# Two chained cross-attention layers on one core: stores between the refills, a first pair by half loads, a later statistics product, and a last attention copy split by bank

## The chip, the cores and the metric

The kernel runs on one core of one Trainium2 chip. The metric is the device time of one launch in microseconds (us). The kernel before took 365.97 us (median of 3 runs, 365.94 to 367.44). Times in the profile come from one further, profiled execution of 364.66 us.

## The reference, cut to what matters

For each of 32 batch elements there are two matrices of 128 channels by 1024 columns, `x` and `y` (the context). Layer 0 is a cross attention in both directions over channels, layer 1 a second one followed by a normalisation over the whole element:

```python
# layer 0, 8 heads of 16 channels; softmax over channels (16 x 16 per head)
attn = softmax(einsum('bhni,bhnj->bhij', q, k) * 16 ** -0.5)
res  = einsum('bhnd,bhde->bhne', v, attn)
x1   = (x + proj_p2r(res_p2r)) + (y + proj_r2p(res_r2p))
# layer 1: queries and keys from y, values from x1
scores = einsum('bhdl,bhel->bhde', Wq y + bq, Wk y + bk) / sqrt(128)
o      = Wo (softmax(scores) (Wv x1 + bv)) + bo + x1
out    = (o - mean(o)) * rsqrt(var(o) + 1e-5) * gn_w[:, None] + gn_b[:, None]
```

Since every attention matrix is channels by channels, the scores need only the 128 x 128 products y·yT and x·yT (summed over the 1024 columns) and the row sums of y. All later weights can then be multiplied together, so that `o` is P·x + Q·y with two 128 x 128 matrices per element.

## The kernel before, in words

The 32 elements are worked on in 16 pairs. One call of `step(h, u, front, middle, back)` on each engine is one step of a pipeline of three parts: **front** transposes the pair's 1024 columns in eight chunks and sums the products in the bank `gacc` (`gram_chunks`, L310); **middle** makes the scores, the softmax and the matrices P and Q of the pair before (`u_products`, `scores`, `z_products`, `m_products`, `pq_products`); **back** forms P·x + Q·y of the pair before that, takes its statistics, normalises it and stores it. Step 0 is (0, 0), step 1 is (0, 1), steps 2 to 15 run in a loop (two to a turn) with all three parts, steps 16 and 17 drain. Each engine has its own instruction order, written out by hand in its `step`; engines meet at semaphores only.

- **SP** issues every DMA, in order, from one queue. There are four slots of buffers (`raw`, `y_blocks`, `xy_hi`, `xy_lo`, `res`); a step uses two. Once a slot's splits and transposes are done, it is refilled with x, four blocks of y, and y for the step after the next (L234 to L247). Both refills come before the two stores of the step (L248 to L259).
- **PE** (TensorE) transposes x (and in step 0 also y) through the bank pair `tpx`; the column chunks of the transposes take every eighth column (L295). In a step, the small product `group_moments` (L352), which averages the statistics over the channels, stands ahead of `m_products` (L414 to L420). PE starts the next pair's `u_products` (L364) when ACT has copied the second `gacc` to `gram`.
- **ACT** (ScalarE) copies the transposes (`xt_out`, L502), `gacc` (`gram_out`, L556), the attention products (`z_out`, L541 and L542), the high part `pq_hi` of P and Q (L547), and the output halves (`out_to_sbuf`, L572); it rounds x and y to their high parts (`split_high`, L565), takes the exponent (L537), makes the scale and shift of the normalisation (`norm_scale`, L524 and L527) and applies it (L586).
- **DVE** (VectorE) transposes the y blocks (L705), does the softmax around the exponent, the statistics (L716 to L764) and the low part `pq_lo` (L709).
- **POOL** (GpSimd) makes the low parts of x and y in pieces (L919) and the power -1/2 of the variance (L926).

For float32 accuracy each output half is made of six products: the high and low parts of x and y with the high part of P and Q, then the high parts with the low part of P and Q.

## Time and profile before

| what | value |
|---|---|
| median of 3 runs | 365.97 us |
| the profiled execution | 364.66 us |
| its span in the trace | 362.9 us |
| PE busy | 334.8 us (92% of the span) |
| PE weight loads busy | 279.7 us (77%) |
| ACT busy | 249.4 us (69%) |
| DVE busy | 243.7 us (67%) |
| POOL busy | 188.8 us (52%) |
| DMA, all queues | 67.43 MB, mean 186 GB/s |
| granted PE clock over the core's span | 0.995 |

How to read it: the span runs from the first to the last recorded instruction; what is missing to the execution's time lies around it. PE is the engine that is busy nearly all the time, so the time can be read as a sum of what PE does and of the places at which it stands idle. "L297" is line 297 of the kernel. In a timeline a row's second number is busy time; since instructions overlap in the pipeline, two neighbours may overlap by some tens of nanoseconds, and differences are best taken from start to start.

### The profile page before, as it was taken

To read this page: it belongs to the slowest core of one execution; us is meant where nothing else is said; L and a number is where in the kernel's file an instruction comes from. 1 tells how busy PE (TensorE), PEld (TensorE's weight loads), DVE (VectorE), ACT (ScalarE), POOL (GpSimd) and SP (SyncE) were. 2 spreads that over 40 slices of the span, in tenths; PEclk is the share of its full clock that TensorE was granted. 3 is DMA by queue.
4 is the path that set the end of the run, shared out by engine and by line. 5 is a ranking of instruction groups with operands and counts; after the bars stand their busy time and mean duration, and the time that the engine had idled before them with its cause. 6 is when DMAs were issued, how large, how long until landed. Compare 5 with 4: busy or idle time off the path is not lost.

```text
span 362.9 us, 8203 instructions
## 1 busy us (share of the span) xinstructions
PE 334.8 (92%) x2646; PEld 279.7 (77%) x2646; DVE 243.7 (67%) x620; ACT 249.4 (69%) x414; POOL 188.8 (52%) x277
## 2 busy tenths in 40 slices
PE   5975999997999999999999999999999999999681
PEld 3864978886797988888897988888797888877470
DVE  1444586774958677694958677694958678593763
ACT  2375486864877787777877786777877686786423
POOL 0079675480845739192846648182845728193001
PEclk9999999999999999999999999999999999999997
DMA  7765545557575565657575665656575756302023
GB/s 246 259 176 167 162 145 166 175 175 271 174 267 173 205 211 151 240 168 268 173 269 175 232 210 170 232 162 246 174 269 175 269 177 220 134 0 116 2 104 128
DMA packets 30410, 67.43 MB, mean 186 GB/s; under 512 B 2368, under 2 KB 17984, under 8 KB 30400
## 3 DMA queue, kind: packets, MB, share of 16 engines
q1 hardware_dynamic: 30400, 67.30, 55.5%
q8 instruction: 5, 0.08, 0.1%
q14 instruction: 5, 0.04, 0.0%
HBM read 50.52 MB, written 16.78 MB: 185 GB/s over the span
## 4 chain that ended last, share of the span: by engine, by line
PE 56%; DVE 16%; SPq 13%; issue 5%; DMA 4%; POOL 3%; ACT 2%; POOLq 0%; DVEq 0%; ACTq 0%
PE gacc L320 19%; SPq L214 8%; PE oacc L340 5%; PE oacc L345 5%; PE oacc L341 5%; PE tpx L297 4%; DVE hstat L716 4%; SPq L208 4%; PE mid L428 3%; POOL xy_lo L919 3%; PE mid L364 3%; DVE mom L740 3%; DMA out<-res 2%; DVE t L705 2%; PE mid L414 2%
## 5 line engine op out<-in xcount | busy, mean ns | idle before, releaser
L919 POOL TENSOR_TENSOR xy_lo<-raw,xy_hi 128x256 fp32r<-128x256 f32 x256 | 177.7, 733 | 130.4 <-ACT xy_hi L565 130.4
L320 PE MATMUL gacc<-t 128*128 128x257 f32 x512 | 124.9, 386 | 3.2 <-DVE attn L814 2.6
L320 PEld LDWEIGHTS gacc<-t 128*128 128x128 f32 x512 | 92.6, 191 | 17.1 <-DVE attn L814 3.0
L705 DVE STREAM_TRANSPOSE t<-y_blocks 128x512 f32<-128x512 f32 x60 | 68.1, 1135 | 3.0 <-DMA y_blocks<-in_ctx 3.0
L565 ACT ACTIVATE xy_hi<-raw 128x1024 fp32r<-128x1024 f32 x64 | 67.4, 1056 | 3.9 <-DMA raw<-in_ctx 3.9
L340 PE MATMUL oacc<-xy_hi,pq_hi 128*128 128x512 f32 x124 | 51.9, 419 | 4.3 <-ACT res L572 2.2
L572 ACT ACTIVATE res<-oacc 128x512 f32<-128x512 f32 x60 | 35.9, 598 | 21.6 <-DMA out<-res 10.5
L341 PE MATMUL oacc<-xy_lo,pq_hi 128*128 128x512 f32 x124 | 48.8, 394 | 0.0
L716 DVE BATCH_NORM_STATS2 hstat<-res 128x6 f32<-128x512 f32 x60 | 39.4, 678 | 13.9 <-ACT res L572 13.9
L502 ACT ACTIVATE t<-tpx 128x512 f32<-128x512 f32 x64 | 38.2, 598 | 12.7 <-PE tpx L297 11.9
L297 PEld LDWEIGHTS tpx<-cst,raw 128*128 128x128 f32 x256 | 36.3, 192 | 4.4 <-DMA cst<-in_consts 1.3
L345 PE MATMUL oacc<-xy_hi,pq_lo 128*128 128x512 f32 x124 | 39.1, 396 | 0.0
L709 DVE TENSOR_TENSOR pq_lo<-mid,pq_hi 128x512 fp32r<-128x512 f32 x16 | 11.1, 692 | 40.7 <-ACT pq_hi L547 40.7
L297 PE MATMUL tpx<-cst,raw 128*128 128x128 f32 x256 | 37.4, 279 | 0.1
L586 ACT ACTIVATE res<-res,nbias,nscale 128x1024 f32<-128x1024 f32 x29 | 35.9, 1238 | 0.5
L340 PEld LDWEIGHTS oacc<-xy_hi,pq_hi 128*128 128x128 f32 x124 | 23.4, 188 | 11.3 <-ACT res L572 2.3
L926 POOL TENSOR_TENSOR rstd<-var,cst 128x2 f32<-128x2 f32 (+1 forms) x17 | 11.5, 675 | 38.6 <-DVE var L764 38.6
L556 ACT ACTIVATE gram<-gacc 128x257 f32<-128x257 f32 x32 | 12.4, 387 | 22.3 <-PE gacc L320 22.3
L345 PEld LDWEIGHTS oacc<-xy_hi,pq_lo 128*128 128x128 f32 x124 | 23.4, 188 | 5.5
L341 PEld LDWEIGHTS oacc<-xy_lo,pq_hi 128*128 128x128 f32 x124 | 23.4, 189 | 4.0
L783 DVE SCALAR_TENSOR_TENSOR u<-wt,gram,mid 128x128 f32<-128x128 f32 x32 | 9.7, 345 | 23.0 <-PE mid L367 23.0
L814 DVE TENSOR_TENSOR attn<-mid,sinv 32x192 f32<-32x192 f32 x64 | 22.4, 351 | 0.7
(101 smaller groups left out, 423.5 us busy)
## 6 DMA issues: line engine op xcount, KB each, us to landing
raw<-in_x SPq DMA_DIRECT2D x32, 512.0 KB, 9.0
raw<-in_ctx SPq DMA_DIRECT2D x32, 512.0 KB, 9.8
out<-res SPq DMA_DIRECT2D x32, 512.0 KB, 8.0
y_blocks<-in_ctx SPq DMA_DIRECT2D x120, 128.0 KB
wt<-in_weights SPq DMA_DIRECT2D x1, 896.0 KB, 7.8
cst<-in_consts SPq DMA_DIRECT2D x1, 147.0 KB, 3.3
w_rot<-in_weights SPq DMA_DIRECT2D x2, 64.0 KB, 7.6
quad<-in_quad_rows SPq DMA_DIRECT2D x1, 32.0 KB, 7.4
```

What stands on the lines that cost most here:

```text
L297: mm = pe.transpose(tpx[i][:, c, :], chunks[:, HC * i + c], ident)
L320: mm = pe.matmul(gacc[:, 0:2 * C + 1], t[slot][:, c, C:2 * C], t[slot][:, c, :], start=(c == 0), stop=(c == CH - 1))
L340: pe.matmul(bank[:, :], whi, xy_hi[slot][:, s, cols], start=(s == 0), stop=False)
L341: pe.matmul(bank[:, :], whi, xy_lo[slot][:, s, cols], start=False, stop=False)
L345: mm = pe.matmul(bank[:, :], pq_lo[u][:, b, s, :], xy_hi[slot][:, s, cols], start=False, stop=(s == 1))
L502: act.activation(t[slot][:, HC * i:HC * (i + 1), 0:C], tpx[i][:, :, :], ACT.Copy)\
L565: act.activation(xy_hi[slot][:, s, :], raw[slot][:, s, :], ACT.Copy).then_inc(split_hi, 1)
L572: act.activation(res[2 * u + b][:, half * HALF:(half + 1) * HALF], oacc[half][:, :], ACT.Copy)\
L586: act.activation(res[2 * u + b][:, :], res[2 * u + b][:, :], ACT.Identity, bias=nbias[:, b:b + 1], scale=nscale[:, b:b + 1]).then_inc(norm ...
L705: dve.transpose(dst, blocks[:, HC * i:HC * (i + 1)]).then_inc(yt_ready, 1)
L716: dve.bn_stats(hstat[:, b, half, :], res[2 * u + b][:, half * HALF:(half + 1) * HALF])\
L919: piece = pool.tensor_tensor(xy_lo[slot][:, s, cols], raw[slot][:, s, cols], xy_hi[slot][:, s, cols].bitcast(f32), ALU.subtract)
```

## The change

Four things are changed, and orders on ACT, DVE and PE with them.

1. **SP**: the two stores of a step are issued between the refill of the first slot and that of the second.
2. **Steps 0 and 1**: the constants are loaded first, and the first element's x and y in two halves each. PE's chunks of the first pair are contiguous columns, so that a half is enough to begin. PE takes the second element's transposes between the two parts of the first one's products. ACT takes its `split_high` calls earlier in step 0, and in step 1 fewer of them ahead of the exponent and of `z_out`.
3. **Loop**: `group_moments` stands behind `m_products`; DVE does the three functions of the variance behind `c_out` instead of ahead of `n12_out`; ACT does `pq_high` ahead of `norm_scale` and the first `normalise`.
4. **Drain**: the attention copy of step 16 is split by bank between ACT and DVE, the last output half of the pair is issued ahead of the wait for the attention, and in step 17 DVE makes the scale and the shift, which ACT made before.

```diff
-            load_x(0, 0)
             sp.dma_start(cst[:, :], consts).then_inc(consts_in, 16)
-            load_y(0, 0)
+            for i in range(2):
+                cols = slice(HALF * i, HALF * (i + 1))
+                sp.dma_start(raw[0][:, 0, cols], x[0][:, cols]).then_inc(x_half_in[i], 16)
+                sp.dma_start(raw[0][:, 1, cols], y[0][:, cols]).then_inc(y_half_in[i], 16)
             load_x(0, 1)
             load_y(0, 1)
...
             def step(h, u, front, middle, back, refill=True):
...
+                if front and refill:
+                    refill_slot(h, u, 0, not middle)
+                if back:
+                    store(h, u, 0, front, middle)
+                    store(h, u, 1, front, middle)
+                if front and refill:
+                    refill_slot(h, u, 1, not middle)
...
-            def m_products(p):
+            def m_products(p, last):
 
                 pe.wait_ge(z_ready, p + 1)
+                if last:
+                    pe.wait_ge(z_bank1_ready, 1)
...
                 if front and not middle:
-                    for b in range(2):
-                        for i in range(2):
-                            x_transpose(h, u, b, i)
-                            y_transpose_first(b, i)
-                        gram_chunks(h, u, b, 0, 4)
-                        gram_chunks(h, u, b, 4, 8)
+                    x_transpose_first(0, 0)
+                    y_transpose_first(0, 0)
+                    x_transpose_first(0, 1)
+                    y_transpose_first(0, 1)
+                    gram_chunks(h, u, 0, 0, 4)
+                    x_transpose_first(1, 0)
+                    y_transpose_first(1, 0)
+                    gram_chunks(h, u, 0, 4, 8)
+                    x_transpose_first(1, 1)
+                    y_transpose_first(1, 1)
+                    gram_chunks(h, u, 1, 0, 8)
...
                     out_half(h - 1, u, 1, 0)
+                    out_half(h - 1, u, 1, 1)
                     z_operands(p - 1)
-                    out_half(h - 1, u, 1, 1)
...
-                if back and front:
-                    group_moments(p - 2)
-                if middle:
-                    m_products(p - 1)
-                if back and middle and not front:
+                if middle:
+                    m_products(p - 1, not front)
+                if back and (front or middle):
                     group_moments(p - 2)
...
+            def z_out_last(p):
+                act.wait_ge(z_done, p + 1)
+                bank = mid[:, 0, 0:3 * C].rearrange("p (s c) -> p s c", c=C)
+                act.activation(z[0:H64, 0, :, :], bank[0:H64, :, :], ACT.Copy)
+                act.activation(z[H64:C, 1, :, :], bank[H64:C, :, :], ACT.Copy).then_inc(z_ready, 1)
...
                 if front and not middle:
-                    for b in range(2):
-                        for i in range(2):
-                            xt_out(h, u, b, i)
+                    xt_out(h, u, 0, 0)
+                    xt_out(h, u, 0, 1)
+                    split_high(h, u, 0, 0, back)
+                    xt_out(h, u, 1, 0)
+                    split_high(h, u, 0, 1, back)
                     gram_out(p, 0)
-                    split_high(h, u, 0, 0, back)
+                    xt_out(h, u, 1, 1)
+                    split_high(h, u, 1, 0, back)
                     gram_out(p, 1)
                     keys_times_sums(p)
-                    split_high(h, u, 0, 1, back)
-                    split_high(h, u, 1, 0, back)
...
+                if middle:
+                    pq_high(p - 1, 1 - u)
+                if back and (front or middle):
                     norm_scale(p - 2)
                     normalise(h - 1, u, 0)
-                if middle:
-                    pq_high(p - 1, 1 - u)
...
+                if front and middle and not back:
+                    split_high(h, u, 0, 1, back)
                 if front and middle:
                     gram_out(p, 1)
...
+            def norm_scale_last(p, b):
+
+                dve.wait_ge(rstd_ready, p + 1 + b)
...
+                dve.tensor_scalar(nscale[:, b:b + 1], rstd[:, b:b + 1], col("gn_w"), None, ALU.mult)\
+                    .then_inc(nscale_ready, 1)
...
+            def z_out_last(p):
+
+                dve.wait_ge(z_done, p + 1)
+                bank = mid[:, 1, 0:3 * C].rearrange("p (s c) -> p s c", c=C)
+                dve.tensor_copy(z[0:H64, 1, :, :], bank[0:H64, :, :])
+                dve.tensor_copy(z[H64:C, 0, :, :], bank[H64:C, :, :]).then_inc(z_bank1_ready, 1)
...
-                if back and front:
-                    moments_out(p - 2)
-                    neg_variance(p - 2, u)
-                    variance(p - 2)
+                if middle and not front:
+                    z_out_last(p - 1)
                 if middle:
                     n12_out(p - 1)
                     n3_out(p - 1)
                     c_out(p - 1, 1 - u)
-                if back and middle and not front:
+                if back and (front or middle):
                     moments_out(p - 2)
                     neg_variance(p - 2, u)
                     variance(p - 2)
```

ACT in the second half of a loop step, before: the copies of `gacc` to `gram`, of `tpx` to `t`, and the rest up to the second `gram`.

```order
94 L556 ACTIVATE gram<-gacc 128x257
95 L499 REGISTER_ALU
96 L502 ACTIVATE t<-tpx 128x4x128
97 L565 ACTIVATE xy_hi<-raw 128x1024
98 L521 ISA
99 L524 ACTIVATE nscale<-rstd,vec 128x2
100 L527 ACTIVATE nbias<-cmu,vec,nscale 128x1 x2
101 L585 REGISTER_ALU
102 L586 ACTIVATE res<-res,nbias,nscale 128x1024
103 L547 ACTIVATE pq_hi<-mid 128x512
104 L551 REGISTER_ALU
105 L556 ACTIVATE gram<-gacc 128x257
```

The same place in the changed kernel:

```order
97 L592 ACTIVATE gram<-gacc 128x257
98 L533 REGISTER_ALU
99 L536 ACTIVATE t<-tpx 128x4x128
100 L604 ACTIVATE xy_hi<-raw 128x1024
101 L583 ACTIVATE pq_hi<-mid 128x512
102 L553 ISA
103 L554 ACTIVATE nscale<-rstd,vec 128x2
104 L557 ACTIVATE nbias<-cmu,vec,nscale 128x1 x2
105 L624 REGISTER_ALU
106 L625 ACTIVATE res<-res,nbias,nscale 128x1024
107 L587 REGISTER_ALU
108 L592 ACTIVATE gram<-gacc 128x257
```

The copy to `pq_hi` has moved ahead of the scale, the two shifts and the first normalisation; these four now stand between it and the second copy of `gacc`.

ACT in step 1, between the copies of the products of `u_products` (`u`) and the attention copies (`z`), before:

```order
8 L533 ACTIVATE u<-mid 128x512
9 L502 ACTIVATE t<-tpx 128x4x128 x2
10 L565 ACTIVATE xy_hi<-raw 128x1024 x2
11 L537 ACTIVATE mid<-mid 128x192
12 L565 ACTIVATE xy_hi<-raw 128x1024
13 L502 ACTIVATE t<-tpx 128x4x128
14 L565 ACTIVATE xy_hi<-raw 128x1024
15 L541 ACTIVATE z<-mid 64x768
16 L542 ACTIVATE z<-mid 64x768
```

The same place in the changed kernel:

```order
11 L563 ACTIVATE u<-mid 128x512
12 L536 ACTIVATE t<-tpx 128x4x128 x2
13 L604 ACTIVATE xy_hi<-raw 128x1024
14 L567 ACTIVATE mid<-mid 128x192
15 L536 ACTIVATE t<-tpx 128x4x128
16 L577 ACTIVATE z<-mid 64x768
17 L578 ACTIVATE z<-mid 64x768
```

One high split instead of two stands ahead of the exponent (`mid<-mid`), and none between it and the attention copies; the three that are gone come later in the step.

## Rows read from the trace of the kernel before

**Rows 1.** Waits of the whole span: who waited for whom, total us, times, longest.

```profile
PEld stat L352 <- DVE mom L740: 7.4, 11, 1.9
...
DVE t L705 <- DMA y_blocks<-in_ctx: 3.0, 2, 2.8
```

**Rows 2.** Chain of waits, two pairs of neighbouring steps: start us, us, what.

```profile
106.79 0.87 PE mid L364 x4
...
126.95 0.87 PE mid L364 x4
...
249.65 0.86 PE mid L364 x4
...
270.40 0.87 PE mid L364 x4
```

**Rows 3.** Timeline of PE, one loop step: start us, busy us, line, out<-in, [idle before].

```profile
266.72 1.05 PE L428 MATMUL mid<-nmat 128*128 128x128 f32 x8
...
269.35 1.05 PE L297 MATMUL tpx<-cst,raw 128*128 128x128 f32 x8
270.24 1.03 PE L364 MATMUL mid<-wt,gram 128*128 128x256 f32 x4
```

**Rows 4.** Timeline of ACT, the same loop step.

```profile
266.82 1.24 ACT L586 ACTIVATE res<-res,nbias,nscale 128x1024 f32<-128x1024 f32 x1
267.97 0.58 ACT L547 ACTIVATE pq_hi<-mid 128x512 fp32r<-128x512 f32 x1
269.55 0.39 ACT L556 ACTIVATE gram<-gacc 128x257 f32<-128x257 f32 x1 [1.01 <-PE gacc L320]
```

**Rows 5.** Timeline of all engines, the first step after the loop.

```profile
331.80 0.39 ACT L556 ACTIVATE gram<-gacc 128x257 f32<-128x257 f32 x1 [1.01 <-PE gacc L320]
...
332.24 1.13 PE L364 MATMUL mid<-wt,gram 128*128 128x256 f32 x4 [0.48 <-ACT gram L556]
...
347.87 0.60 ACT L547 ACTIVATE pq_hi<-mid 128x512 fp32r<-128x512 f32 x1 [3.53 <-PE mid L428]
...
349.39 1.25 ACT L586 ACTIVATE res<-res,nbias,nscale 128x1024 f32<-128x1024 f32 x1
```

**Rows 6.** Timeline of all engines, the first late store.

```profile
82.09 0.92 SPq L259 DMA_DIRECT2D out<-res  x2
...
90.54 0.50 PE L340 MATMUL oacc<-xy_hi,pq_hi 128*128 128x512 f32 x1 [2.17 <-ACT res L572]
```

**Rows 7.** Timeline of all engines, step 1, up to its softmax.

```profile
21.28 1.11 DVE L705 STREAM_TRANSPOSE t<-y_blocks 128x512 f32<-128x512 f32 x1 [2.78 <-DMA y_blocks<-in_ctx]
...
22.74 0.61 DVE L783 SCALAR_TENSOR_TENSOR u<-wt,gram,mid 128x128 f32<-128x128 f32 x2 [0.35 <-PE mid L367]
...
23.52 0.58 ACT L533 ACTIVATE u<-mid 128x512 f32<-128x512 f32 x1
...
25.68 0.37 DVE L795 TENSOR_TENSOR mid<-mid,smax 128x192 f32<-128x192 f32 x1
...
26.85 0.33 ACT L537 ACTIVATE mid<-mid 128x192 f32<-128x192 f32 x1
```

**Rows 8.** Timeline of PE, the end of step 1.

```profile
35.09 0.70 PE L414 MATMUL mid<-z,wt 128*128 128x256 f32 x2 [1.82 <-ACT z L542]
...
41.99 0.81 PE L364 MATMUL mid<-wt,gram 128*128 128x256 f32 x3
```

**Rows 9.** Timeline of all engines, DVE's preparation beside POOL's first work.

```profile
17.22 0.22 DVE L679 TENSOR_SCALAR wt<-wt 128x128 f32<-128x128 f32 x1
...
17.56 0.95 DVE L684 SCALAR_TENSOR_TENSOR mask<-quad,nbq,cst 128x32 f32<-128x32 f32 x2
17.73 1.41 POOL L919 TENSOR_TENSOR xy_lo<-raw,xy_hi 128x256 fp32r<-128x256 f32 x2 [17.28 <-ACT xy_hi L565]
```

**Rows 10.** Timeline of all engines, the last attention copy.

```profile
343.75 0.35 DVE L740 SCALAR_TENSOR_TENSOR mom<-mom,pstat 128x1 f32<-128x1 f32 x2
...
344.39 0.70 PE L414 MATMUL mid<-z,wt 128*128 128x256 f32 x2 [1.74 <-ACT z L542]
```

More of the change, by code:

```diff
@@ new lines, in store @@
+            def store(h, u, b, front, middle):
+                q = 4 * h + 2 * u + b - 4
+                if front:
+                    sp.wait_ge(normed, q + 3)
+                elif middle:
+                    sp.wait_ge((normed, last_normed)[b], (q + 3, 1)[b])
+                else:
+                    sp.wait_ge(normed, q + 2)
+                    if b == 1:
+                        sp.wait_ge(last_normed, 2)
+                sp.dma_start(out[q], res[2 * u + b][:, :]).then_inc(stored[2 * u + b], 16)
@@ L562, in split_high @@
                 act.wait_ge((x_in, y_in)[s][slot], 16 * (h + 1))
+                if isinstance(n, int) and n == 0:
+                    for half in range(2):
+                        act.wait_ge((x_half_in, y_half_in)[s][half], 16)
                 if s == 0 and back:
@@ L612, in step @@
                     out_to_sbuf(h - 1, u, 0, 1)
-                if front and middle:
                     split_high(h, u, 0, 0, back)
@@ L620, in step @@
                     out_to_sbuf(h - 1, u, 1, 0)
-                if front and middle:
+                if back and front:
                     split_high(h, u, 0, 1, back)
@@ L626, in step @@
                     xt_out(h, u, 1, 0)
+                if back and front:
                     split_high(h, u, 1, 0, back)
-                if middle:
+                if front and middle:
                     z_out(p - 1)
+                if middle and not front:
+                    z_out_last(p - 1)
                 if front and middle:
@@ L647, in step @@
                     keys_times_sums(p)
+                if front and middle and not back:
+                    split_high(h, u, 1, 0, back)
+                    split_high(h, u, 1, 1, back)
                 if back and not front and not middle:
-                    norm_scale(p - 2, slice(0, 1), True)
                     normalise_last(h - 1, u, 0, range(2))
-                    norm_scale(p - 2, slice(1, 2), True)
                     normalise_last(h - 1, u, 1, range(1))
@@ L871, in step @@
                     y_transpose(h, u, 1, 1)
-                if back and front:
-                    moments_out(p - 2)
-                    neg_variance(p - 2, u)
-                    variance(p - 2)
+                if middle and not front:
+                    z_out_last(p - 1)
                 if middle:
@@ L879, in step @@
                     c_out(p - 1, 1 - u)
-                if back and middle and not front:
+                if back and (front or middle):
                     moments_out(p - 2)
```

102 lines of the change are left out of this document (57 added, 45 removed).

## The prediction, made before the changed kernel was run

> **What bounds the kernel now.** I read the table of busy times first: PE is busy for 92% of the span, so I look for PE's idle places, and for what would make new ones. The table of waits has one that repeats: PE's weight load for the statistics product waits for DVE's `mom`, 11 times, 7.4 us [rows 1]. The chain of waits then gives the loop's period, from one `u_products` to the next. A step in which PE waits for nothing takes 126.95 - 106.79 = 20.16 us, one with the statistics wait 270.40 - 249.65 = 20.75 us [rows 2]. From the first such product of step 2 at 41.99 to the one after the loop at 332.24 there are 290.25 us for 14 steps, 20.73 on average [rows 5, 8]. One single wait stands out: the stores of step 2 are issued at 82.09, behind both refills of their step, and PE is held 2.17 us in step 4, since ACT may not overwrite `res` [rows 6]. Ahead of the loop step 1 is bound by latency: PE stands 1.82 us for ACT's attention copy [rows 8].
>
> **Step 1.** Before, ACT starts the exponent at 26.85, though its operand was done at 25.68 + 0.37 = 26.05; it was in two high splits. Now one split stands ahead, which is over in time: 0.80 us. The scores waited for ACT's copy of `u`, 23.52 + 0.58 = 24.10, also behind splits. What is left in its place is DVE: the transpose of the y blocks cannot start before they land at 21.28, then `u3` takes 0.61 and a second transpose 1.1, so that the masking comes some 0.9 us earlier; one more DMA is issued ahead of the blocks, for which I take 0.2 off: 0.7 us [rows 7]. Behind the exponent no split stands before the attention copy, so PE's 1.82 us at L414 go [rows 8]. Together 0.80 + 0.7 + 1.82 = 3.3; with a little of the weight load's own start I take 3.4 us. The three splits that ACT does later lie beside PE's products: one of them stands between `pq_hi` and the second `gacc` copy, which PE wants only 3.52 us after L428 [rows 3], and the last two behind that copy, where PE has two output halves to do before it wants `u`. The early loads (constants first, halves) bring PE's first products forward by 1 to 1.5 us, and I count nothing for it: the landing of the blocks at 21.28 hides it. That is the cover; if the blocks landed earlier, up to 1 us more would come. Ends for step 1: 0.8 + 1.8 = 2.6 and 3.4 + 1.0 = 4.4. The product after step 1 comes at 41.99 - 3.4 = 38.6.
>
> Preparation on DVE now runs while POOL works, as POOL's first pieces come some 8 us earlier. The rows show the two last instructions of it at 0.95 us together, beside POOL's first pieces of 0.7 each, against 0.22 for a larger instruction just before [rows 9]; so two of them are held up for a piece each, 1.4 us, which the landing of the blocks hides too. The Trainium skill, "SBUF — State Buffer", section "Who interferes with whom", says more: one-input copies and `tensor_scalar` in SBUF take the port pair that DVE shares with GpSimd as well, and the loser blocks for a whole instruction. By that rule all seven larger instructions of the preparation would be held up, 7 x 0.7 = 4.9 us, and the sum would be 0.3 us higher. No row of before shows such a `tensor_scalar` beside POOL.
>
> **The loop.** I follow PE from its last middle products (L428) to the next `u_products`, in before: 266.72 to 270.24, 3.52 us, of which none is a wait, for ACT copies the second `gacc` at 269.55 and ends 0.30 us before PE wants it [rows 3, 4]. The statistics product moves behind the five products of `m_products`. They cover the mean wait of 7.4 / 11 = 0.67 us [rows 1], so the wait goes and none follows in its place. The price is on ACT. `pq_hi` waits for PE's L428 (1.05 us and about 0.04 to ACT) [rows 3]. Behind it now stand scale, two shifts and the first normalisation: from the start of `pq_hi` to that of the normalisation it takes 349.39 - 347.87 = 1.52 us in the step after the loop, which has this order already [rows 5]; the normalisation holds ACT for 267.97 - 266.82 = 1.15 us [rows 4]; the copy of `gacc` and the signal to PE take 332.24 - 331.80 = 0.44 us [rows 5]. Sum 1.05 + 0.04 + 1.52 + 1.15 + 0.44 = 4.20 us, against 3.52 for PE alone: PE waits 0.68 us in every step for ACT's `gram`. Before, ACT did scale and normalisation in the gap before `pq_hi`, in which it now stands idle, because DVE does the variance behind `c_out`, and by its own order cannot release POOL's power much before `pq_done`. So the period is 20.2 + 0.7 = 20.9 us in all steps, where it was 20.16 to 20.75: the move takes out a wait of about 0.6 us and puts in one of 0.7. I take 14 x 20.9 = 292.6 us against 290.25, +2.35, and the 2.17 us of the late store are already gone in that sum, because the stores of step 2 are issued one refill earlier, and they were late by less than that. If `gram` weren't late, it would be 14 x 20.2 = 282.8 (-7.5); if all 1.15 + 0.1 us of the normalisation came on top, 14 x 21.4 = 299.6 (+9.3). The value is near the middle, from rows that show the same instructions in the same order.
>
> The stores between the refills put 0.9 us of issue [rows 6] ahead of the second slot's refill, and the wait for the second normalisation with it. Who waits behind it are only the loads for the step after the next; SP issues the stores of step 2 only at 82.09, which is in step 4, so the normalisations are long done when it comes to them, and the cost is nothing as long as a step takes longer than SP's issue of it.
>
> **The drain.** The last attention copy holds PE 1.74 us, until 344.39. PE now does the last half before the attention wait, but DVE's share of the copies stands behind its statistics, which end at 343.75 + 0.35 = 344.10 [rows 10]. They come about 1.1 us earlier, since the half they wait for does, and two copies of 384 columns at some 0.5 each (0.58 for ACT's 512 columns [rows 7]) end at 344.0: -0.4. Ends: 0 and -1.74. Scale and shift on DVE in step 17 save a change of engine twice but hold DVE ahead of its last `bn_stats`; +0.1 in all. Drain -0.3.
>
> **Sum.** -3.4 + 2.35 - 0.3 = -1.35 on the profiled execution of 364.66 (span 362.9 and 1.76 around it): 363.3. The median of the runs lies 1.3 above that execution. In before, how many of the steps have the statistics wait depends on timing, and two more of them would be these 1.2 us; the changed loop has one kind of step. So I add 0.5: 363.8 us, 0.6% under 365.97. A measurement of this kernel tells about 0.5%, 1.8 us, from no change, so the line for faster is 364.1.
>
> **Rivals.**
> - *The `gram` copy isn't late, or less so.* ACT's gap before it was 1.01 us [rows 4], and the work that comes in is longer than that; this speaks against it. Half of the wait gives 363.8 - 4.8 = 359.0, none of it 354.
> - *Half of the start is lost.* The blocks land later than at 21.28, or PE waits in step 2 or 3 for blocks that SP's queue brings no earlier than now. Price 1.7: 365.5. For it: SP issues without a pause in this stretch. Against: POOL's low parts, for which the refills wait, are earlier too.
> - *Slower.* The transfers hold PE where they hold it now: the 3.4 us won in step 1 are given back in steps 2 and 3, where DVE waits for `y_blocks`, and a wait like the 2.78 us at 21.28 [rows 7] is added. It decides from the point at which the blocks land later than 3.4 us before DVE wants them. The loop's +2.35 stays. 363.8 + 3.4 + 1.4 (half of that wait) = 368.6.
>
> **How the numbers follow.** Forecast, 0.58: own range 362.3 to 365.3, split by the line at 364.1 into 0.33 faster and 0.25 within 0.5%. The first rival 0.17, all faster. The second 0.13, within. The slower one 0.12. Faster 0.50, within 0.38, slower 0.12. The range 360.0 to 366.8 leaves out most of the first rival and the slower one.
>
> **What would show it.** In the changed profile: the loop's period even, near 20.9; a PE wait of 0.5 to 0.7 at `u_products`, released by ACT's `gram`, 14 times, and none at the statistics product; no wait of ACT for a store; `u_products` of step 2 near 38.6; ACT idle about 3 us before `pq_hi`. Wrong would be a period near 20.2 (first rival), waits of DVE for `y_blocks` in steps 2 to 4 (the others), or a first `u_products` of step 2 later than 40.

## The result, and the profile of the changed kernel

The changed kernel takes 373.33 us (median of 20 runs, 365.83 to 376.95), the kernel before 365.85 us (20 runs on the same chip). The ratio is 1.0066 with a 95% interval of 1.0036 to 1.0097. The change makes the kernel slower; I had said 363.8 and faster. Ratios in this document compare only the runs within 1.5% of a kernel's fastest, while medians take all runs, so the changed kernel's median lies 2.0% above that of before and its profiled execution (374.94 us, span 373.1 us) is one of its slower ones.

The busy table and the slices of the page come first. PE was busy for 92% of the span before too; what is new stands in the row PEclk, a 7 in the seventh slice and a run of 6s at the end.

```profile
PE 342.9 (92%) x2646; PEld 285.7 (77%) x2646; DVE 255.0 (68%) x628; ACT 246.8 (66%) x410; POOL 189.0 (51%) x277
...
PE   7969968999999999999999999999999999998591
...
POOL 0833973372738366372738366472738365470001
PEclk9999997999999999999999999999999999999667
```

The waits of PE, by what released them (us in total, times, longest):

```profile
PE mid L393 <- ACT gram L592: 7.6, 14, 1.4
PE stat L381 <- DVE mom L787: 4.6, 2, 2.7
PE mid L445 <- DVE z L830: 3.2, 1, 3.2
...
PE mid L450 <- DVE abv L884: 1.3, 1, 1.3
```

The first row is the wait that I had forecast at `u_products`, in place of the 11 of [rows 1]: 13 times 0.48 us, and 1.37 us at the last. The third is the wait for the last attention copy, which the drain of my prediction implies in one piece too. The second and the fourth are not in it. Timeline of PE, the first `u_products` of steps 2, 3, 4 and 5, to be held against [rows 2, 8]:

```profile
37.94 1.03 PE L393 MATMUL mid<-wt,gram 128*128 128x256 f32 x4
...
65.36 0.92 PE L393 MATMUL mid<-wt,gram 128*128 128x256 f32 x3 [0.48 <-ACT gram L592]
...
86.27 1.13 PE L393 MATMUL mid<-wt,gram 128*128 128x256 f32 x4 [0.48 <-ACT gram L592]
...
107.18 1.13 PE L393 MATMUL mid<-wt,gram 128*128 128x256 f32 x4 [0.48 <-ACT gram L592]
```

Step 2 comes early, at 37.94 (41.99 before), and then lasts 27.42 us. From 65.36 on every step takes 20.91 us, to the last `u_products` at 337.24, and the end takes 373.1 - 337.24 = 35.9 us (362.9 - 332.24 = 30.7 before). The whole miss splits in three, measured on the profiled execution, for which I had forecast a span of 361.5:

| part | forecast | measured | miss |
|---|---|---|---|
| to the `u_products` of step 2 | 38.6 | 37.94 | -0.7 |
| step 2 | 20.9 | 27.42 | +6.5 |
| the 13 steps behind it | 271.7 | 271.88 | +0.2 |
| the end | 30.4 | 35.9 | +5.5 |

**Step 2.** Timelines of POOL, DVE and PE:

```profile
37.12 16.60 POOL L985 TENSOR_TENSOR xy_lo<-raw,xy_hi 128x256 fp32r<-128x256 f32 x24 [1.40 <-ACT xy_hi L604]
```

```profile
47.23 6.51 DVE L884 TENSOR_TENSOR abv<-abv_s,sinv 128x2 f32<-128x2 f32 x1
53.67 1.09 DVE L752 STREAM_TRANSPOSE t<-y_blocks 128x512 f32<-128x512 f32 x1
...
56.47 0.35 DVE L787 SCALAR_TENSOR_TENSOR mom<-mom,pstat 128x1 f32<-128x1 f32 x2
```

```profile
53.80 0.38 PE L450 MATMUL mid<-abv,wt 128*128 128x2 f32 x2 [1.27 <-DVE abv L884]
56.87 0.59 PE L381 MATMUL stat<-mom,cst 128*128 128x4 f32 x2 [2.69 <-DVE mom L787]
57.32 3.77 PE L349 MATMUL gacc<-t 128*128 128x257 f32 x8
```

`abv`, a product of two numbers per partition, took 6.51 us, and it ended at 53.74, when POOL's 24 pieces did (37.12 + 16.60 = 53.72). PE stood for it, and again for `mom`. A long burst of POOL is not new in itself. The kernel before has one of 28 pieces, but it lies in step 1; that step's `abv` passes in it in 0.32 us, and step 1 has no statistics of a pair before it. Timelines of POOL and DVE, before:

```profile
22.75 19.27 POOL L919 TENSOR_TENSOR xy_lo<-raw,xy_hi 128x256 fp32r<-128x256 f32 x28 [2.23 <-ACT xy_hi L565]
```

```profile
29.34 0.32 DVE L818 TENSOR_TENSOR abv<-abv_s,sinv 128x2 f32<-128x2 f32 x1
```

In the changed kernel three high splits of step 1, with four pieces each, come last in their step and join the 12 pieces of step 2's first three splits. Those are the 24, and they lie beside step 2's attention and statistics.

Behind the two waits PE runs at a lower clock: the same eight products of 257 columns took 3.77 us instead of the 1.99 that they take at full clock. The granted clock, by windows (us, busy of PE, PEld, DVE, ACT, POOL, PEclk, DMA share, GB/s), step 2 and the end:

```profile
36.00:50.00 14.00, 14.00 (x128) 11.45 (x127) 10.37 (x19) 12.26 (x21) 12.88 (x19) 1.00 0.56 171
50.00:54.00 4.00, 2.73 (x18) 2.35 (x16) 4.00 (x2) 2.45 (x4) 3.73 (x6) 1.00 0.47 154
54.00:58.00 4.00, 1.31 (x6) 1.13 (x6) 3.86 (x11) 0.00 (x0) 0.00 (x0) 0.58 0.70 207
58.00:62.00 4.00, 4.00 (x16) 3.35 (x15) 1.66 (x8) 0.00 (x0) 2.23 (x4) 0.56 0.32 101
...
349.00:353.00 4.00, 3.55 (x12) 3.13 (x12) 0.93 (x3) 0.00 (x0) 0.00 (x0) 0.50 0.00 0
353.00:357.00 4.00, 2.92 (x10) 2.53 (x11) 1.78 (x8) 1.45 (x4) 0.69 (x1) 0.50 0.01 2
357.00:361.00 4.00, 4.00 (x10) 3.05 (x10) 1.51 (x2) 1.24 (x1) 0.00 (x0) 0.50 0.48 194
```

0.50 is the lower of the clock's two levels, 1.2 GHz. In step 2 it is reached at about 54.7 us, inside a stretch from 52.5 to 56.9 in which PE stands idle for 1.27 and 2.69 us, with two small products between. At the end it is reached in the idle piece of 3.24 us, at about 348.2, and lasts until 361.9.

**The end.** Timelines of DVE, ACT and PE, for [rows 10]:

```profile
345.22 1.87 DVE L763 BATCH_NORM_STATS2 hstat<-res 128x6 f32<-128x512 f32 x3
...
348.02 0.55 DVE L829 COPY z<-mid 64x384 f32<-64x384 f32 x1
348.59 0.56 DVE L830 COPY z<-mid 64x384 f32<-64x384 f32 x1
```

```profile
346.62 0.48 ACT L573 ACTIVATE z<-mid 64x384 f32<-64x384 f32 x1
```

```profile
345.17 0.89 PE L436 MATMUL mid<-wt,attn 64*64 64x128 f32 x24
349.30 1.19 PE L445 MATMUL mid<-z,wt 128*128 128x256 f32 x2 [3.24 <-DVE z L830]
```

ACT's half of the copy was over at 347.10; DVE's ended at 349.15, behind three `bn_stats` and the moments. Counted from `u_products`, `m_products` starts at 12.06 us, before at 344.39 - 332.24 = 12.15. So the wait itself costs nothing against before, where PE stood in two shorter pieces, 1.36 and 1.74 us, with work between them. The price is behind it: 23.8 us from `m_products` to the end instead of 18.5, with the clock at 0.50 where it was 1.00.

### The profile page after: what moved, and what is told of

Same layout as the page of the kernel before. It is cut to its first block, busy times and chain, and to the rows that moved or that the text cites. A ratio compares the mean times of both kernels' runs of the same rounds, so it can differ in the third digit from the quotient of the medians.

```text
span 373.1 us, 8210 instructions
## 1 busy us (share of the span) xinstructions
PE 342.9 (92%) x2646; PEld 285.7 (77%) x2646; DVE 255.0 (68%) x628; ACT 246.8 (66%) x410; POOL 189.0 (51%) x277
## 4 chain that ended last, share of the span: by engine, by line
PE 68%; issue 10%; SPq 7%; DVE 6%; ACT 5%; DMA 3%; POOLq 0%; POOL 0%; ACTq 0%; DVEq 0%
PE gacc L349 20%; PE oacc L369 8%; PE oacc L374 7%; PE oacc L370 7%; PE mid L393 4%; PE mid L459 4%; SPq L217 4%; PE tpx L308 3%; PE mid L436 3%; DMA y_blocks<-in_ctx 3%; PE mid L445 2%; PE mid L446 2%; PE mid L396 2%; ACT nbias L557 2%; SPq L208 2%
## 5 line engine op out<-in xcount | busy, mean ns | idle before, releaser
L349 PE MATMUL gacc<-t 128*128 128x257 f32 x512 | 127.2, 391 | 2.7 <-DVE attn L880 1.9
L349 PEld LDWEIGHTS gacc<-t 128*128 128x128 f32 x512 | 93.8, 193 | 17.1 <-issue 2.6
L369 PE MATMUL oacc<-xy_hi,pq_hi 128*128 128x512 f32 x124 | 52.9, 426 | 0.8 <-ACT pq_hi L583 0.7
L370 PE MATMUL oacc<-xy_lo,pq_hi 128*128 128x512 f32 x124 | 49.7, 401 | 0.0
L583 ACT ACTIVATE pq_hi<-mid 128x512 fp32r<-128x512 f32 x16 | 9.6, 597 | 57.5 <-PE mid L459 57.5
L374 PE MATMUL oacc<-xy_hi,pq_lo 128*128 128x512 f32 x124 | 39.9, 403 | 0.0
L308 PEld LDWEIGHTS tpx<-cst,raw 128*128 128x128 f32 x240 | 33.6, 191 | 3.0
L308 PE MATMUL tpx<-cst,raw 128*128 128x128 f32 x240 | 34.0, 274 | 0.0
L393 PE MATMUL mid<-wt,gram 128*128 128x256 f32 x64 | 17.9, 402 | 7.6 <-ACT gram L592 7.6
```

The source lines that it names most:

```text
L308: mm = pe.transpose(tpx[i][:, c, :], chunks[:, HC * i + c], ident)
L349: mm = pe.matmul(gacc[:, 0:2 * C + 1], t[slot][:, c, C:2 * C], t[slot][:, c, :], start=(c == 0), stop=(c == CH - 1))
L369: pe.matmul(bank[:, :], whi, xy_hi[slot][:, s, cols], start=(s == 0), stop=False)
L370: pe.matmul(bank[:, :], whi, xy_lo[slot][:, s, cols], start=False, stop=False)
L374: mm = pe.matmul(bank[:, :], pq_lo[u][:, b, s, :], xy_hi[slot][:, s, cols], start=False, stop=(s == 1))
```

## The experiments

All were run beside the kernel before on the same chip, in four groups; its medians there were 366.13, 365.46, 365.54 and 365.63 us. The table has the median, the ratio to before with its interval, and from the profiled execution of each the start of step 2, its length, the period behind it, and the end (from the last `u_products`). One execution of each was profiled. The loop's period is steady; step 2 and the clock at the end differ from run to run of one kernel, so a part of one profile is not the part of the median.

| kernel | median | ratio | step 2 at | lasts | period | end |
|---|---|---|---|---|---|---|
| before (its own 20 runs) | 365.85 | | 41.99 | 20.75 | 20.73 mean | 30.7 |
| changed, again | 375.04 | | 38.12 | 26.77 | 20.91 | 32.4 |
| z copies on ACT | 368.37 | 1.001 (0.998-1.005) | 37.45 | 24.15 | 20.91 | 33.2 |
| abv_s in PSUM | 369.66 | 1.006 (1.002-1.010) | 39.73 | 22.53 | 20.94 | 32.3 |
| abv_s and pstat in PSUM | 368.79 | 1.008 (1.005-1.011) | 37.30 | 20.83 | 20.93 | 32.4 |
| splits of step 1 back | 370.48 | 1.011 (1.006-1.016) | 42.88 | 20.84 | 20.92 | 34.8 |
| DVE's z copies first | 371.11 | 1.016 (1.013-1.020) | 36.75 | 26.87 | 20.92 | 33.0 |
| z on ACT and earlier | 370.83 | 1.016 (1.011-1.021) | 38.86 | 27.41 | 20.91 | 30.7 |
| gram copy first | 359.74 | 0.979 (0.974-0.984) | 37.59 | 23.52 | 20.16 | 36.2 |
| before + loop order | 367.97 | 1.003 (0.999-1.007) | 40.84 | 20.77 | 20.90 | 30.6 |
| before + end | 368.30 | 1.007 (1.004-1.010) | 40.39 | 20.76 | 20.75 | 34.2 |
| before + SP order | 364.01 | 0.994 (0.990-0.998) | 41.73 | 20.74 | 20.75 | 30.6 |
| before + start + SP | 365.17 | 1.000 (0.997-1.003) | 44.94 | 20.74 | 20.75 | 30.6 |
| before + SP + PSUM | 359.64 | 0.975 (0.970-0.980) | 41.72 | 20.18 | 20.20 | 34.7 |
| same + start + splits | 354.69 | 0.969 (0.965-0.974) | 37.11 | 24.05 | 20.19 | 34.7 |
| changed, all causes out | 354.61 | 0.966 (0.962-0.970) | 39.10 | 20.19 | 20.21 | 34.9 |

### Is the result repeatable?

The changed kernel, unchanged, once more.

> The changed kernel again, unaltered, for a second trace and the spread. Theory (two stalls, each followed by the 1.2 GHz level): the loop's period from step 3 on is 20.91 us in every execution; what differs between executions is whether DVE's small product for abv in step 2 is held for several POOL pieces (6.5 us in the first trace) and whether PE's wait of 3.2 us for the last attention copy is followed by half clock. Executions with mean clock 0.99 lie near 365 to 366, with 0.97 near 373. Rival (transfers): DVE's waits for y_blocks in steps 1 and 2 (7.0 us in all) differ between executions and set the time; the clock is a by-effect.

375.04 us (6 runs): the long step 2 (26.77; `abv` held for 7.12 us) and the period are there again, so they belong to the kernel. The end took 32.4 us, its wait 3.24 again, but the clock stayed at 1.00 for 5 us behind it and was at 0.50 for only some 3 us. This execution took 371.04 us. Its miss against the forecast splits into -0.5, +5.9, +0.2 and +2.0. So step 2 is the larger part of the miss in both, and what the end costs differs by 3.5 us between two executions of the same kernel.

### The end: the copies on ScalarE, earlier, or DVE's first

Both copies on ACT (and no wait of PE for `z_bank1_ready`):

```diff
-                if front and middle:
+                if middle:
                     z_out(p - 1)
-                if middle and not front:
-                    z_out_last(p - 1)
```

> The last attention copy is made by ACT alone again (both banks), with the changed order of the output half kept. Theory: DVE's statistics no longer stand ahead of the copy, so PE's wait at the first m_product of step 16 falls from 3.2 us to about 1.8 (two copies of 0.81), the clock stays at 2.4 GHz through the drain, and 5 to 6 us go (from u_products of step 16 to the end 30 us instead of 36). The step-2 loss of 6.5 us stays where it occurs. Rival (transfers or chance set the clock): the drain is as slow as before, 35 to 36 us.

The wait fell from 3.24 to 1.74, yet the clock was at 0.50 for some 10 us behind it and the end took 33.2, which is less than the 35.9 of the first profile and more than the 32.4 of the repeat. So the gain in the median, 6.7 us, can't be put down to the end. Step 2 took 24.15 in this one. There `abv` took 0.23, and it was the first instruction of `mom` that was held, 2.36 us, until POOL's burst was over. Which instruction is held varies from run to run.

The kernel before with only this part of the change:

> The kernel before with only the step behind the loop changed as the change does it (last attention copy by bank on ScalarE and VectorE, last products of the scale and shift on VectorE). If the VectorE half is what makes the end long, TensorE waits 3.2 us at m_products of the last step instead of 1.4 to 1.7, and the drain from the last u_products grows from 30.7 to 32.5 (35.9 where the granted clock falls to 0.5 behind the wait): median 366.1 + 1.5 to + 5, so 367.6 to 371. If the end is long only because of the order of the loop (moments behind m_products), the wait stays at 1.7 and the median within 0.5 of 366.1.

+0.72% (0.44 to 1.01), as the first theory has it: this part of the change costs time by itself. The last attention's rows of PE are those of the changed kernel, and so is the clock behind them:

```profile
339.54 0.89 PE L408 MATMUL mid<-wt,attn 64*64 64x128 f32 x24
343.67 1.19 PE L417 MATMUL mid<-z,wt 128*128 128x256 f32 x2 [3.24 <-DVE z L792]
```

```profile
343.00:345.00 2.00, 1.33 (x3) 1.17 (x4) 0.52 (x1) 0.00 (x0) 0.00 (x0) 0.50 0.00 0
...
349.00:351.00 2.00, 1.31 (x5) 0.92 (x4) 0.70 (x2) 1.46 (x5) 0.00 (x0) 0.50 0.00 0
```

DVE's two copies put ahead of its last three `bn_stats` in the changed kernel:

```diff
+                if middle and not front:
+                    z_out_last(p - 1)
                 if back and middle and not front:
                     half_stats(h - 1, u, 0, 1)
...
-                if middle and not front:
-                    z_out_last(p - 1)
                 if middle:
                     n12_out(p - 1)
```

> The changed kernel with VectorE's two z copies of the last attention put ahead of the last three bn_stats and the moments instead of behind them. If the place behind 2.9 us of statistics is what makes TensorE wait 3.24 us, the wait falls to 1.0 to 1.5, less than the 1.7 that ScalarE alone took, and the drain of 32.4 to 35.9 falls by 2 or more (it keeps the clock of 1.0 if the length of the wait decides that, and it stays at 0.5 for some us if the order of the products ahead of it does): median 375.0 less 2 to 5. If the copies are late for another reason the wait stays at 3 us.

The wait fell to 1.3 us, the lowest of all, so the place behind the statistics is what made it long. But the end still took 33.0, no less than in the repeat, with the clock at 0.50 from 350 to 356.8, although no idle piece of PE before it was over 1.34 us. A short wait alone does not keep the clock. The median is in the range that I gave; the end did not bring it there.

Copies on ACT and the attention's products back ahead of the last output half, as before the change:

```diff
                     out_half(h - 1, u, 1, 0)
+                    z_operands(p - 1)
                     out_half(h - 1, u, 1, 1)
-                    z_operands(p - 1)
```

> The changed kernel with the copies of the last attention on ScalarE alone and its products put back ahead of the last output half, so that 1.1 us of output products run while it is copied. Against the run with the copies on ScalarE alone (368.4, where the granted clock still fell to 0.5 for some 8 us behind a wait of 1.7): if it was the gap behind the attention's products with no work left that took the clock, the clock stays at 1.0 through the last products and the end takes 30.7 instead of 33.2, median 366 (365 to 367). If the copies' engine alone matters, the clock falls again and the median is 368 to 369.

The end took 30.7, with the clock at 1.00 through the last products:

```profile
350.00:354.00 4.00, 3.08 (x20) 2.69 (x20) 1.81 (x8) 0.47 (x2) 0.67 (x1) 1.00 0.01 2
354.00:358.00 4.00, 3.64 (x16) 2.98 (x17) 2.77 (x4) 2.40 (x5) 0.02 (x1) 1.00 0.18 72
```

So the profile is what the first theory says, and the median of 370.8 is not. It lies 4.8 us over the 366 that I said: step 2 had its full 27.41 here, 3.3 more than in the kernel from which I took the sum, and the rest I did not separate. That the end of before keeps the clock is no rule either. In the three profiles below with a loop of 20.2 us PE has the same two idle pieces (1.08 to 1.36 and 1.74 us, with the half between them), the clock falls to 0.50 for 10 us all the same, and the end takes 34.7 to 34.9. In the other direction, the seven profiles with the end of the change show a wait of 3.0 to 3.24 us and an end of anything from 32.3 to 36.2. What decides on the clock behind the wait stays open.

### Step 2: what holds DVE

`abv_s` kept in PSUM, so that `abv` reads one operand from SBUF:

```diff
-        abv_s = sb("abv_s", [C, 2])
+        abv_s = stat[:, 8:10]
```

> The sum abv_s lies in PSUM, so that DVE's product for abv has one SBUF input instead of two; nothing else. Theory (DVE waits for the SBUF port that POOL holds): that product takes 0.2 us in all steps, also in step 2; steps 2 to 3 take 20.9 to 21.5 us instead of 27.4, without the half clock, 5 to 6.5 us gained where it occurred. Rival (transfers): the product isn't the cause, step 2 stays at 27 us or the wait moves to the next DVE instruction with two SBUF inputs (mom).

`abv` took 0.16 in all 16 steps, and step 2 fell to 22.53, short of the first theory's range. As the second half of the rival says, the hold moved to the next instruction with two operands in SBUF, again to the end of the burst (38.91 + 16.65 = 55.56):

```profile
48.46 0.16 DVE L884 TENSOR_TENSOR abv<-stat,sinv 128x2 f32<-128x2 f32 x1
52.13 3.45 DVE L783 TENSOR_TENSOR mom<-pstat,cshift 128x2 f32<-128x2 f32 x1
```

With `pstat` in PSUM too (`pstat = stat[:, 10:14]`, seen as [C, 2, 2]):

> The changed kernel with abv_s and pstat kept in PSUM, so that abv, the mean's sum and the second moment each read at most one operand from SBUF. If the long hold of step 2 falls on whichever two-operand VectorE instruction meets GpSimd's burst, none of these is over 0.5 us any more, the statistics product no longer waits 1.5 to 2.7, and step 2 is 20.9 to 22.0 (27.4 in the changed kernel, 22.5 with abv_s alone): the loop and the end are unchanged, median 375.0 - 5.5 to - 7 = 368 to 369.5. If the hold only moves on again (attn, transposes, N matrices), step 2 stays at 22.5 or more and the median at 369.7 or more.

Step 2 took 20.83, though POOL's burst is as long as ever. Timelines of DVE and POOL:

```profile
46.07 0.16 DVE L884 TENSOR_TENSOR abv<-stat,sinv 128x2 f32<-128x2 f32 x1
50.68 0.16 DVE L783 TENSOR_TENSOR mom<-stat,cshift 128x2 f32<-128x2 f32 x1
50.88 0.34 DVE L787 SCALAR_TENSOR_TENSOR mom<-mom,stat 128x1 f32<-128x1 f32 x2
```

```profile
36.48 16.65 POOL L985 TENSOR_TENSOR xy_lo<-raw,xy_hi 128x256 fp32r<-128x256 f32 x24 [1.39 <-ACT xy_hi L604]
```

That settles it: the second operand in SBUF beside a burst of POOL, not the burst alone. (The median, 368.79, is 4.5 to 6.3 us under the two of the changed kernel.) The rest is where the burst comes from. With the four high splits of step 1 where the kernel before has them:

> The changed kernel with the four high splits of step 1 put back where the kernel before has them. If step 2 is long because those splits were late and left GpSimd a backlog of 24 pieces beside the attention's small VectorE products, the abv product is back under 0.8 us, no VectorE operation is held over 2 us in step 2, and that step falls from 27 to 21 to 22 us; step 1 grows by what the splits take from ScalarE's path (17.6 to between 18.5 and 20.8); median 375.0 less 3 to 6, so 369 to 372. If the shorter start itself or the transfers make step 2 long, it stays at 26 us or more and the median above 373.

POOL's pieces then come in two groups of 12 with a pause of 8.9 us, `abv` takes 0.73 us, the two instructions of the second moment 1.3 together, and step 2 takes 20.84. But step 1 grew by 5 us, from 17.6 to 22.55, more than the 3.2 that I allowed: PE waits 3.3 us at L445 for the attention copy, which stands behind the splits again, and the clock was at 0.50 from 34.1 to 37.5. The late splits were what made step 1 short, and they were what put the burst beside step 2's statistics; the one came with the other.

The start and SP's order alone, on the kernel before:

> The changed kernel with only its start (first pair from half loads) and SP's order kept: step 1's splits, the order in the loop and the copies of the last attention are as before. If the start's gain is real and separable, u_products of step 2 stands at 38.0 to 41.0 (before 41.99) and all later steps take 20.8, drain 30.7: median 366.1 - 2.2 (late store) - 1.0 to -3.5 = 360.4 to 362.9. If the start pays for itself by a longer step 2 even so, step 2 is 23 us or more and the median is 364 or more.

Neither as it stands. The median is the rival's, but step 2 is no longer than before (20.74); it is step 1 that took 24.46, so that `u_products` of step 2 stood at 44.94, and the ratio is 1.000. Without the moved splits the half loads bring nothing. ACT waits 5.49 us for the load of a split and starts this split at 31.10; in the kernel before it starts at 31.04, after 3.87 us. The attention copy stands behind it in both, PE waits 3.4 us for that, and the clock is at 0.50 from 34.3 to 41. So before's wait at L414 hung on a load as well as on ACT's work, and moving the splits takes it out of that wait.

### The stores

> The kernel before with only SP's order changed (each pair's stores between the refills of the two slots). If the order of the stores is a plain gain, the 2.17 us wait for the late store goes and nothing else moves: u_products of step 5 comes 20.9 us after that of step 4 instead of 23.12, step 2 stays at 20.75, median 364.0 (ratio 0.994). If the new order makes the later refills late (the rival for the long step 2), some step grows by 1 us or more by a wait for x, y or y_blocks, and the median is 366 or more.

0.994 (0.990 to 0.998): a small gain, and of the parts tried alone the only one. ACT's wait for a late store is gone and all steps take 20.75. Yet in the profiles the loop is no shorter: from step 3 to the last `u_products` it takes 331.96 - 62.47 = 269.49, before 332.24 - 62.74 = 269.50. Behind the late store of [rows 6] the kernel before had five steps of 20.16 to 20.34, in which `mom` was no longer late; the 2.17 us came back in them. Why the median is 1.5 us lower all the same stays open.

### The loop

The new order alone, on the kernel before:

> The kernel before with only the order of the loop changed: statistics product behind m_products, variance behind c_out on DVE, pq_hi ahead of the scale on ACT. Both theories: the period becomes 20.9 us in every step (before 20.16 to 20.75), PE waits 0.5 to 0.7 us at u_products for ACT's gram; +2.3 us on the whole if the late store of step 4 (2.2 us) goes with nothing, more like +3 to +4.5 if that wait stays: 367 to 370 against 365.9.

The period is 20.87 to 20.92 (but for one of 21.85 with the late store) with PE's wait of 0.48 at `u_products`, as expected. The ratio is 1.003 (0.999 to 1.007), which by itself isn't clear of no change.

The changed kernel with the second `gram` copy ahead of both normalising passes:

```diff
                     norm_scale(p - 2)
+                if front and middle:
+                    gram_out(p, 1)
+                if back and (front or middle):
                     normalise(h - 1, u, 0)
...
-                if front and middle:
-                    gram_out(p, 1)
```

(step 1's split, which stood between them, now stands ahead of the scale.)

> The changed kernel with one difference on ScalarE in the loop: the second gram copy stands behind the scale and ahead of both normalising passes, instead of behind the first of them. If the 0.48 us for which TensorE waits at u_products is what lengthens the loop from 20.76 to 20.91, the wait goes and the period is 20.3 to 20.5 in the 13 steps, 375.0 less 13 x 0.4 to 0.6 = 367 to 370. If another wait takes its place (ScalarE late for the y products or the out halves), the period stays at 20.7 or above and the median within 2 of 375.

The median is 359.74, lower than either theory has it, 13.6 us under the changed kernel's 373.33. The period is 20.16: 13 x 0.75 = 9.8 us, where I had allowed 0.4 to 0.6 per step. Step 2 gave some 3.9 more: it took 23.52, as `abv` passed in 0.66 and `mom` was held for 1.57. That part is luck of the execution, not the moved line: which instruction is held, and how long, varies. Timelines of ACT and PE, first the changed kernel, then this one:

```profile
229.59 0.60 ACT L583 ACTIVATE pq_hi<-mid 128x512 fp32r<-128x512 f32 x1 [2.85 <-PE mid L459]
...
231.10 1.24 ACT L625 ACTIVATE res<-res,nbias,nscale 128x1024 f32<-128x1024 f32 x1
232.25 0.36 ACT L592 ACTIVATE gram<-gacc 128x257 f32<-128x257 f32 x1
...
232.66 1.13 PE L393 MATMUL mid<-wt,gram 128*128 128x256 f32 x4 [0.48 <-ACT gram L592]
```

```profile
221.69 0.39 ACT L592 ACTIVATE gram<-gacc 128x257 f32<-128x257 f32 x1 [0.27 <-PE gacc L349]
221.97 2.36 ACT L625 ACTIVATE res<-res,nbias,nscale 128x1024 f32<-128x1024 f32 x2
...
222.37 1.03 PE L393 MATMUL mid<-wt,gram 128*128 128x256 f32 x4
```

The copy now waits for PE's `gacc` and not for ACT's own queue. With this one copy moved, the change is a gain of 2% (1.6 to 2.6).

Was the 20.75 of before a hold by POOL too? Before with SP's order and the two operands in PSUM:

> The kernel before with only SP's order changed and abv_s and pstat in PSUM: start, order in the loop and end as before. If the wait for the statistics (some 0.6 us per step at 20.75) comes from VectorE's moments being held beside GpSimd, and not from the place of the product, the period is 20.15 to 20.2 with the product where it always stood, 13 x 0.6 = 7.5 less than with SP's order alone: 364.0 - 7.5 = 356.5 (355.5 to 357.5), and the kernel with the new start too (354.7) is then ahead by what the start is worth, 1 to 2. If the period stays at 20.75, the 20.19 of that kernel came from the start or the splits, and the median is 363.5 to 364.5.

Yes: the period is 20.20 with the statistics product where it always stood, against 20.75 with SP's order alone. The two instructions of the second moment took 1.33 us together beside POOL in the kernel before, and take 0.34 now (`abv` too takes 0.16 instead of 0.73; the two operands were moved together, so their shares aren't known):

```profile
261.73 1.33 DVE L740 SCALAR_TENSOR_TENSOR mom<-mom,pstat 128x1 f32<-128x1 f32 x2
```

```profile
214.73 0.16 DVE L743 TENSOR_TENSOR mom<-stat,cshift 128x2 f32<-128x2 f32 x1
214.93 0.34 DVE L747 SCALAR_TENSOR_TENSOR mom<-mom,stat 128x1 f32<-128x1 f32 x2
```

The median, 359.64, is 3 above what I expected. The six runs lie in two groups, 355.1 to 358.6 and 360.7 to 361.6; the profiled one is of the second, and in it the clock was at 0.50 for some 10 us of the end, which took 34.7.

### What is best

> The kernel before with SP's order, the start and the high splits of steps 1 and 2 from the changed kernel, abv_s and pstat in PSUM; order in the loop and the step behind it as before. If only the hold spoiled the new start, u_products of step 3 stands at 20.4 + 17.6 to 19.0 + 20.8 to 22 = 58.8 to 61.4 (62.5 with SP's order alone), the loop runs at 20.75 and the end takes 30.7: median 364.0 - 1 to - 3.5 = 360.5 to 363. If the shorter start is given back in steps 1 and 2 by other waits, the median is 364.0 or more, no better than with SP's order alone.

> The changed kernel with the gram copy ahead of both normalising passes, abv_s and pstat in PSUM, and the step behind the loop as in the kernel before. Each of the three causes taken away at once: step 2 at 20.8 to 21.5 as with PSUM alone (27.4 in the changed kernel), steps 3 to 15 at 20.15 as with the early gram copy (20.91), the end in 30.7 (35.9). Sum: 58.2 for u_products of step 3, + 12 x 20.15 + 19.9 + 30.7 = 350.6, + 1.8 = 352.4. If the causes overlap (the early gram copy costs step 2 as in the run with it alone, 23.5), the median is 354.5 to 357.

354.69 and 354.61, some 11 us (3.1 and 3.4%) under before and lower than every other kernel; the two don't differ by more than their intervals. The first lies 6 us under its range, which took the loop at 20.75, while PSUM made it 20.19. It has a step 2 of 24.05: nothing is held, but DVE waits 2.69 us for `y_blocks`, PE then 1.93 for `mom`, and the granted clock is 0.62 on average in 53 to 57. In the second the statistics product stands behind `m_products`, PE waits for nothing in step 2, and it takes 20.19. So in these two executions step 2 is shorter with the order of the change. The second kernel's sum came out at 354.6 and not at 352.4: its fastest run took 352.4, and in the profiled one the clock at the end was at 0.50 for some 10 us and the end 34.9 instead of 30.7.

## Why the prediction was wrong

**The start: right, by its own steps.** 38.6 was said and 37.94 measured, L445 with no wait in step 1. That it came so near is in part luck: in the ten profiles with the new start and the moved splits this product stands at 36.8 to 39.7, in the five with before's start at 40.4 to 42.0. In the preparation beside POOL three of the four `tensor_scalar` took 0.76 us each instead of 0.22, and it was hidden, as I said. The Trainium skill, "SBUF — State Buffer", section "Who interferes with whom", has it that a `tensor_scalar` in SBUF can contend with GpSimd; this trace agrees.

**"The three splits that ACT does later lie beside PE's products": the step that failed.** I priced them on ACT and PE alone, at nothing. Each high split releases four POOL pieces of 0.7 us, and so the moved splits put 12 pieces directly ahead of step 2's 12, 24 without a pause beside `abv` and `mom`. I wrote in "what would show it" only of ACT and `y_blocks`. The same section of the Trainium skill also says that a DVE instruction with two SBUF inputs contends with a GpSimd instruction that reads SBUF, and that one with at most one, outside the modes that use two ports, does not; I had it open for the preparation and did not carry it to `abv` and `mom`. The runs agree with both halves of the rule: 6.51 us for two operands in SBUF, 0.16 with one in PSUM. Price: 6.5 us (5.9 in the repeat), of which 1.27 + 2.69 are waits of PE and 1.8 are the eight products at the lower clock.

**The loop: right in mechanism and size.** 20.9 said, 20.91 measured; the wait at `u_products` is 0.48 on PE and 0.67 on its weight load in 13 steps (1.37 and 1.77 in the last), where I had 0.68, and the statistics wait has gone from the loop. "If `gram` weren't late: 14 x 20.2" was the right price of that case too, as the run with the copy first shows. I took before's 0.6 us per step as a matter of the product's place. It was DVE held beside POOL, and PSUM takes it out as well.

**"Drain -0.3", with two copies that "end at 344.0: -0.4": wrong in size and sign.** I let DVE's copies begin at 344.10 less 1.1, so 343.0 on before's clock. In after they begin at 348.02, which is 343.0 + 5.0, just there; and PE starts `m_products` 12.06 behind `u_products` instead of the 11.8 forecast. So the times of DVE were right. What I left out is the clock: I took the products behind the wait at full speed. In this execution the piece of 3.24 us was followed by 13 us at 1.2 GHz, 5.3 us from there to the end and 5.5 with the rest; in the repeat by 3 us, and the end missed by 2.0. That the end as changed costs time is shown by the run with it alone (+0.7%). Why is only argued. The last output half, moved ahead of the attention's products, had been the work that parted PE's two idle pieces, and the run with the products put back ended in 30.7 us at full clock; but three kernels with the very pieces of before fell to 1.2 GHz as well. So what brings the clock down there stays open.

**The stores: the wait went as said** (though 82.09 is not in step 4, as I wrote, but at the end of step 3, for PE starts step 4 at 83.51), but the gain in the loop is not the 2.17 us of it, as above. My sum had counted it within the period, so this cost the forecast nothing.

**The rivals.** The slower one had a chance of 0.12 and another mechanism, `y_blocks`; DVE did wait 7.0 us for them, and in one experiment a wait for them made step 2 3.9 us longer than its best, but here another thing held first. I had no rival on POOL at all, and none on the clock, and those two are what put the time above the 366.8 at which the range ended.

## What to carry to other kernels

When work that feeds GpSimd is moved, lay GpSimd's new busy stretch over VectorE's small two-operand instructions: their price can be not their own length but the rest of the burst (here up to 7.1 us), and one operand in PSUM took it away. At a place where TensorE is short of work, count what the granted clock may cost behind the gap, read it in more than one execution, and don't take one trace for the price. Where a queue gets work in front of a copy that TensorE waits for, try the copy in front of that work first: here that was worth 10 us in the loop.

## What had not been expected of the hardware

A VectorE instruction of 0.16 us was held for 6.51, 6.73, 6.98 and 7.12 us in four executions, always to the end of GpSimd's run of 24 pieces of 0.7 us: it did not get its turn between two pieces. In two others the same instruction passed in 0.23 and 0.66 us in the midst of such a burst, and `mom` was held instead (2.36 and 1.57 us), again to its end. In the loop's shorter bursts it takes some 0.73 us. So a held instruction can lose to many in a row, or to one; what decides it stays open, and so does how often it happens, since two of the changed kernel's executions were profiled and its runs spread from 365.83 to 376.95 us. And with a loop of 20.2 us the clock at the end fell to 0.50 in the profiled executions even with the end of before (34.7 to 34.9 us against 30.7), though no idle piece of TensorE there was over 1.74 us; why is open too.
